# Spreading the attention values from SBUF to SBUF in sixteen transfers per group, from a value tile held twice, instead of writing them to DRAM and reading them back

## The reference

```
def reference(x, subjects, ..., conditions, ...):
    y = einsum('bct,bcd->bdt', x, w_mix1[subjects])         # 128 x 32 x 256
    q, k, v = bitlinear(y, wq), bitlinear(y, wk), bitlinear(y, wv)   # 16 heads of 16
    attn = softmax(where(causal, q @ k.T / sqrt(16), -inf))  # 32 x 32 for each head
    x = x + bitlinear((attn @ v).reshape(B, S, D), wp)
    z = einsum('bct,bcd->bdt', x, w_mix2[conditions])
    gates = top-2 of softmax(z @ router_w), normalised
    return x + sum over the two chosen experts e of
               gate_e * ((silu(z @ gate_w[e]) * (z @ up_w[e])) @ down_w[e])
```

## Time and profile before

| | |
|---|---|
| median of 3 runs | 494.92 us (494.81 to 497.31) |
| profiled execution, its own time | 493.43 us |
| its span in the profile | 491.7 us |
| TensorE busy | 341.8 us (70%) |
| VectorE busy | 261.6 us (53%) |
| ScalarE busy | 245.1 us (50%) |
| GpSimd busy | 236.3 us (48%) |
| mean granted clock of TensorE | 0.876 |

### The profile page before, as it was taken

How to read it: one execution, slowest core, us unless ns; L and a number is a source line. 1 busy time by engine, 2 the same in 40 slices (tenths; PEclk the granted TensorE clock), 3 DMA queues, 4 the chain that set the end, 5 groups by cost and what they waited for, 6 DMA issues and landing times.

```text
span 491.7 us, 11060 instructions
## 1 busy us (share of the span) xinstructions
PE 341.8 (70%) x3257; PEld 255.5 (52%) x3257; DVE 261.6 (53%) x913; ACT 245.1 (50%) x580; POOL 236.3 (48%) x248
## 2 busy tenths in 40 slices
PE   0456989989989897958755407988789888981000
PEld 0342647666756566645544306777677767760000
DVE  1635587978869797955744462333233423331531
ACT  9152778866869585845642303454444444440000
POOL 3651231246445555463556361555455555555672
PEclk9977999998999999998965657999899989997555
DMA  6506465365362715353557265544354434413994
GB/s 218 142 3 158 64 154 135 57 131 135 78 185 50 206 44 146 80 144 72 142 147 204 92 245 141 157 128 142 108 149 140 149 119 137 143 33 144 326 381 173
DMA packets 76897, 68.87 MB, mean 140 GB/s; under 512 B 41003, under 2 KB 65968, under 8 KB 76721
## 3 DMA queue, kind: packets, MB, share of 16 engines
q1 hardware_dynamic: 65200, 44.03, 36.0%
q0 software_dynamic: 7296, 20.02, 11.2%
q10 hardware_dynamic: 4352, 4.20, 2.5%
HBM read 35.36 MB, written 30.62 MB: 134 GB/s over the span
## 4 chain that ended last, share of the span: by engine, by line
PE 45%; DVE 17%; issue 9%; DMA 6%; another core or an unknown queue 5%; POOL 5%; ACT 5%; DVEq 4%; SPq 1%; POOLq 0%; ACTq 0%
PE bank L1355 12%; PE bank L1366 7%; DMA arena<-y_d 4%; PE bank L1348 3%; PE bank L1193 3%; PE bank L1244 2%; PE bank L1270 2%; PE bank L1221 2%; PE bank L1127 2%; PE bank L1142 2%; POOL arena L549 2%; DVE stats L898 2%; PE bank L1232 2%; DVE amax L851 2%
## 5 line engine op out<-in xcount | busy, mean ns | idle before, releaser
L542 POOL DMA_INDIRECT y_d<-cen,di x79 | 77.8, 985 | 77.7 <-ACT cen L748 54.0
L1057 DVE SCALAR_TENSOR_TENSOR kT<-kT,hrow,bank 128x96 f32<-128x96 f32 x79 | 24.8, 314 | 98.4 <-ACT kT L743 72.9
L502 POOL DMA_INDIRECT routed<-hrow,posi x64 | 62.8, 982 | 26.7 <-issue 16.8
L1355 PE MATMUL bank<-arena,qT 128*128 x316 | 68.6, 341 | 7.3 <-ACT qT L738 7.3
L491 POOL TENSOR_TENSOR sc<-sc,mx 128x512 f32<-128x512 f32 x32 | 33.6, 1051 | 82.1 <-DVE mx L880 82.0
L1355 PEld LDWEIGHTS bank<-arena,qT 128*128 128x128 f32 x316 | 51.4, 196 | 11.7 <-issue 11.6
L748 ACT ACTIVATE cen<-bank 128x256 f32<-128x256 f32 x79 | 30.6, 387 | 44.7 <-PE bank L1366 33.2
L1366 PE MATMUL bank<-arena,sc 96*128 x158 | 51.3, 408 | 2.0 <-issue 1.0
L1348 PE MATMUL bank<-ident,hrow 128*128 128x128 f32 x158 | 31.9, 285 | 24.5 <-DMA hrow<-routed 19.4
L738 ACT ACTIVATE qT<-bank 128x256 f32<-128x256 f32 x79 | 30.5, 386 | 22.9 <-PE bank L1348 22.7
L1348 PEld LDWEIGHTS bank<-ident,hrow 128*128 128x128 f32 x158 | 23.0, 148 | 33.8 <-DMA hrow<-routed 19.8
(11 more groups left out here) (169 smaller groups left out, 752.9 us busy)
## 6 DMA issues: line engine op xcount, KB each, us to landing
hrow<-routed SPq DMA_DIRECT2D x79, 129.0 KB
arena<-y_d SPq DMA_DIRECT2D x16, 512.0 KB, 5.4
v_d<-v_sb SPq DMA_DIRECT2D x8, 544.0 KB
vx<-v_d SPq DMA_DIRECT2D x32, 136.0 KB
X<-in_x SPq DMA_DIRECT2D x8, 512.0 KB
arena<-kT SPq DMA_DIRECT2D x64, 64.0 KB
out_x<-X ACTq DMA_DIRECT2D x16, 256.0 KB, 5.5
arena<-in_L_ffn_gate_w SPq DMA_DIRECT2D x4, 384.0 KB
```

The source lines that it names most:

```text
L502: g_.indirect_dma_start(routed, bass.IndirectOffsetOnAxis(ap=posi[g % 2][:, t, k:k + 1], axis=0), hrow[:, g % 2, t, k, :], None).then_inc( ...
L542: g_.indirect_dma_start(y_d, bass.IndirectOffsetOnAxis(ap=di[:, n:n + 1], axis=0), ye[n], None, bounds_check=Y_ROWS - 1, oob_is_err=False) ...
L1057: v.scalar_tensor_tensor(out=hh[n % 2], in0=sg[n % 2], scalar=xe[n][:, D + 1:D + 2], in1=bank[2 + n % 2][:, F:2 * F], op0=ALU.mult, op1=AL ...
L1355: last = t_.matmul(bank[2 + n][:, 0:2 * F], xeT[n][:, c, :], gu[:, c, bass.ds(expert[m + LAG - 1], 1), :].rearrange("p o f -> p (o f)"), s ...
```

## The change

The DRAM tensor `v_d`, `put_v` and its semaphore `v_put` go. `v_sb` is held twice, and group g uses `v_sb[g % 2]`. `spread_v(g)` waits for `copy_v` of its own group and for `attend(g - 1, 3)`, and then copies from `v_sb` to `vx` directly. A transfer now takes one sequence position b of a tile and one slot s, for the group's four tiles, so there are 4 x 4 = 16 of them, each of 32 x 4 x 68 numbers (34 KB). `copy_v` no longer waits for `put_v` of the group before, but for the spread of the group two before. GpSimd clears one more tile at the start.

```diff
-    v_sb = sb("v_sb", [P, TG, H, VW])
+    v_sb = [sb(f"v_sb{i}", [P, TG, H, VW]) for i in range(2)]
...
-            def put_v(g):
+            def spread_v(g):
                 if absent(g):
                     return
                 wait(sp, v_copied, g, 2, 2)
-                wait(sp, vx_in, g, 16 * SLOTS, 16 * SLOTS, lag=1)
-                sp.dma_start(v_rows, v_sb[:, :, :, :].rearrange("p t h r -> p t (h r)")).then_inc(v_put, 16)
-
-            def spread_v(g):
-                if absent(g):
-                    return
                 if g == 0:
                     sp.wait_ge(vxz_ok, 1)
-                wait(sp, v_put, g, 16, 16)
                 wait(sp, o_ready, g, TG, TG, lag=1)
-                for s in range(SLOTS):
-                    sp.dma_start(vx[s * SEQ:(s + 1) * SEQ, :, s, :], v_slots[s]).then_inc(vx_in, 16)
+                for b in range(BT):
+                    for s in range(SLOTS):
+                        sp.dma_start(vx[s * SEQ:(s + 1) * SEQ, b:TG * BT:BT, s, :],
+                                     v_sb[g % 2][b * SEQ:(b + 1) * SEQ, :, s * SLOTS:(s + 1) * SLOTS, :].rearrange("p t h r -> p t (h r)")).then_inc(vx_in, 16)
 
             def iteration(it):
-                put_v(it - 1)
                 spread_v(it - 1)
                 load_bd1(it + 2)
                 load_bd2(it - 1)
                 spread_k(it)
...
-            g_.memset(v_sb[:, :, :, :], 1.0)
+            for i in range(2):
+                g_.memset(v_sb[i][:, :, :, :], 1.0)
...
-                wait(act, v_put, g, 16, 16, lag=1)
+                wait(act, vx_in, g, 16 * SLOTS * BT, 16 * SLOTS * BT, lag=2)
...
-                    wait(pe, vx_in, g, 16 * SLOTS, 16 * SLOTS)
+                    wait(pe, vx_in, g, 16 * SLOTS * BT, 16 * SLOTS * BT)
```

More of the change, by code:

```diff
@@ L73, in build_in @@
     mix_d = [nc.dram_tensor(f"mix{i}_d", [BATCH, SEQ * SEQ], fp32, kind="Internal").ap() for i in range(2)]
-    v_d = nc.dram_tensor("v_d", [GT, H * VW], fp32, kind="Internal").ap()
     routed = nc.dram_tensor("routed", [E * PITCH, ROW], fp32, kind="Internal").ap()
@@ L202, in build_in @@
     q_ready, q_copied, k_ready, k_scaled, v_ready, v_copied = [sem(n) for n in ("q_ready", "q_copied", "k_ready", "k_scaled", "v_ready", "v_copied")]
-    kx_in, v_put, vx_in = sem("kx_in"), sem("v_put"), sem("vx_in")
+    kx_in, vx_in = sem("kx_in"), sem("vx_in")
     sc_ready, sc_copied, mx_ok, sub_ok, exp_ok = [sem(n) for n in ("sc_ready", "sc_copied", "mx_ok", "sub_ok", "exp_ok")]
@@ L277, in build_in @@
     x_v = x.rearrange("(t b) s d -> (b s) t d", b=BT)
-    v_rows = v_d.rearrange("(t p) r -> p t r", p=P)
-    v_slots = v_d.rearrange("(n j) (s r) -> s j n r", j=SEQ, s=SLOTS)
     with nc.Block() as block:
@@ L635, in copy_v @@
                     t = 2 * n + k
-                    last = a_.activation(v_sb[:, t, :, 0:HD], src[:, k * D:(k + 1) * D].rearrange("p (h r) -> p h r", h=H), ACT.Copy, scale=s_v[:, t:t + 1])
+                    last = a_.activation(v_sb[g % 2][:, t, :, 0:HD], src[:, k * D:(k + 1) * D].rearrange("p (h r) -> p h r", h=H), ACT.Copy, scale=s_v[:, t:t + 1])
                 last.then_inc(v_copied, 1)
```

## The result

The changed kernel takes 502.33 us (median of 9 runs, 498.78 to 511.4), the kernel before 497.77 us on the same chip (9 runs, 494.81 to 503.54): 1.0095 of it, with a 95% interval of 1.0062 to 1.0127. It is slower by about 1%, where no measurable change was forecast.

A forecast was written before the change was run, and what follows sets the result against it. No engine was near full, so chains of waits were taken as the limit. Span 491.7 - 5.9 (gain) + 3.9 (loss) = 489.7, plus 3.2 for a median of 492.9 us, no measurable change; range 486 to 500.

The forecast's parts named there:

- the gain: Iterations 4 to 8: without the write to `v_d`, stalls of TensorE under nearly full DMA engines shrink, 5.9 us.
- rival 2: Iterations 4 to 9: the write to `v_d` doesn't hold TensorE, gain 0, 3.9 us lost, 498.8 us; chance 0.12.
- rival 1: SP's queue: sixteen issues become the path, +9.7 us at 0.83 us an issue, 504.6 us; chance 0.15.
- The loss: SP's sixteen issues make group 1, group 7 and the first keys late: 2.0 + 1.2 + 0.7 = 3.9 us.
- An issue of SP: SP's queue: each of the sixteen transfers takes 0.71 us, with 0.47 and 0.83 as the ends.
- Keys of group 1: Iteration 1: the keys' spread, queued behind the sixteen in SP, begins at 56.3 against 55.59, 0.7 us late.
- `attend(1, 0)`: Group 1: landing takes 13.1 us from 62.44 where 11.1 are there, so it is late by 2.0 us.
- Landing: End of each set of sixteen: 2.4 us from the start of the last transfer to the work waiting for it.
- Keys of group 2: Iteration 2: issued 3.5 us late, but their scores had 3 us to spare and move by 2.0 anyway: nothing.
- Groups 2 to 6: Middle groups: 13.6 to 14.5 us are there for the values, in time by 0.7 us, no loss.
- Group 7: Its first `attend`: values late by 1.9 us, of which 1.2 count, as transposes behind wait 0.70 for ScalarE.
- Clearing: Program start: GpSimd's clearing of a second `v_sb`, 1.01 us, fits in 3.02 us idle and costs nothing.

The follow-up runs named there:

- before_again: The kernel before, run again unchanged for a second profile: 492.5 us (one run).
- write_too: The changed kernel with the old write of the values to `v_d` put back, which nothing reads: 503.44 us, 1.0156 of the kernel before.
- after_again: The changed kernel, run again unchanged on another chip: 501.63 us, 1.0022 of the kernel before.
- s_dram_first_two: The changed kernel with scatters apart, groups 0 and 1 through DRAM, second value tile cleared late: 477.23 us, 0.9634 of the kernel before.
- four_of_16: The changed kernel, groups 1 to 7 issuing only the first four of their sixteen transfers: 500.52 us, 1.0067 of the kernel before.
- s_clear_late: The changed kernel with scatters apart and the second value tile cleared in iteration 0: 481.08 us, 0.9708 of the kernel before.
- spaced_after: The changed kernel with GpSimd's scatters apart: 482.05 us, 0.9772 of the kernel before.
- two_ahead: The kernel before with scatters apart, except scatter 0 (two DMAs) put ahead of `rstd_x`: 474.63 us, 0.9604 of the kernel before.
- dram16: The kernel before, still through DRAM, with the values read back in sixteen transfers instead of four: 503.41 us, 1.0141 of the kernel before.
- s_sbuf_first_two: The changed kernel with scatters apart, second tile cleared late, only groups 0 and 1 from SBUF, the rest through DRAM: 477.73 us, 0.9644 of the kernel before.
- keys_clear: The changed kernel with the keys' spread issued ahead of the `bd` blocks and the second tile cleared in iteration 0: 504.63 us, 1.0140 of the kernel before.

## Why the prediction was wrong

Its sum was -5.9 + 3.9 = -2.0 us, for a time of 492.9 us and a range from 486 to 500; by the medians the change costs 4.6, and the time is 502.33.

**The step that failed is the gain.** It rested on one reading, that TensorE is held "while the DMA engines are nearly full", and the stall in iteration 7 is the same at a DMA share of 0.35. The write to `v_d` was priced at 1.8 us of the stall in iteration 7, 2.9 of that in 8 and 0.4 in each of 4 to 6. Measured 0 in iterations 7 and 8: 2.42 and 6.41 without the write, 2.44 and 6.42 with it; in 4 and 5 the pieces are 2.41 and 2.29 without, 2.34 and 2.18 with it. This was rival 2 (498.8 us), given 0.12; the time came out between it and rival 1 (504.6), but rival 1's condition, 0.78 us or more for an issue, wasn't met. The write was the only large transfer there, and its issue coincided with the empty 3.8 us; but the window was cut to begin there: the piece itself begins at 214.46, 2.4 us before the write is issued at 216.84 (212.83 and 215.21 in before_again). And that window had only GpSimd's scatters busy, four of the six in a row, and they were set aside as what "go on beside it". Putting them apart gave 21.8 us (495.3 to 473.54). In terms of the prediction: what the stall follows is the row of scatters, and no share of it is the write's. Whether the write costs something elsewhere is open (see write_too), but taking it away gave no gain in any run, with the scatters in rows or apart.

**The loss was right in kind and too small.**
- An issue of SP: 0.71 us taken, 0.602 the median of 128 in after_again, with gaps and stretched ones (up to 1.75) 10.3 to 11.5 us a set (12.0 at most in write_too); 11.4 forecast. Right.
- Keys of group 1: 0.7 us late forecast. They are issued 2.1 late (57.67 against 55.59), and TensorE waits 2.65 instead of 0.71. The spread began at 42.79 and not at 41.10, where the old write stood: the first scores of group 0 were already 1.5 us late (44.41 against 42.88). The clearing may have a share in it; how much, the runs don't tell.
- `attend(1, 0)`: 2.7 late with the keys' share forecast, 4.3 measured (77.82 against 73.54). The set was said to start when `vx` is free, 62.44; SP was still in keys and x until 64.4.
- Landing 2.4 us behind the start of the last issue: in s_dram_first_two SP's set ends at 222.07, its last issue began some 0.6 earlier, and the waiting `attend` starts at 223.93, 2.5 behind. Right.
- Keys of group 2, "nothing": right, the scores of group 2 wait for the `attend` ahead of them.
- Groups 2 to 6, nothing: right with the scatters apart. In the changed kernel itself their stretch is 2.6 to 4.7 us longer, for a reason that isn't known, but not by waits for their values. Group 7, 1.2: measured 1.4 with the scatters apart.
- Clearing "costs nothing": it costs 0.83 us of VectorE; first scores of group 0 start at 43.57 to 44.41 in the kernels with both clearings ahead, and at 42.96 to 43.41 in those with the second one late. But kernels with only one tile to clear have them at 42.80 to 43.97, so a price for the clearing doesn't come out of these.
- Left out altogether: the fall of the granted clock behind most of these waits (0.58 and 0.85 of full speed from 64 to 76 us in after_again). Its price is small where a later wait takes it up: in four_of_16, where `attend(1, 0)` doesn't wait, it comes 10.87 us after the first scores, against 10.39 and 10.22 before, so 0.5 to 0.7 us.

The two parts add up as far as the noise lets one see: 3.2 + 2.7 us, 5.9 of the 6.5 lost in s_clear_late, of which the rows explain 1.4 at group 7 (of the 2.7) and the late keys and `attend(1, 0)`. Why spaced_after, on another chip, shows 8.5 instead, and the change with the scatters in rows 4.6, isn't settled.

The best version is spaced, the kernel before with GpSimd's scatters apart: 0.956 [0.9508, 0.9612]. With it the way through DRAM is still the better one.

## What to carry to other kernels

A transfer that is issued where a stall stands needn't be its cause: compare the two starts first (here the stall began 2.4 us before the issue), and before pricing a gain on it, put the transfer back, or take it away alone, and look whether the stall moves. When a change adds issues to a queue that serves several stages, write out when that queue is free, issue by issue, from what stands ahead of it in the same iteration, and not from when the buffer is free. Where a change adds a wait of about 2 us or more to TensorE, price it once with the slower matmuls behind it and once without: here they followed in seven profiles of eight.

## What the runs showed of the hardware

- Four indirect scatters of GpSimd in a row (0.96 us each, 4.8 in all) go with a stop in the chain of waits of 2.2 to 2.4 us in iterations 4 to 7, six in a row (7.3 in all) with one of 6.3 to 7.6 in iteration 8 (before, before_again, after, after_again, write_too). It ends 1.0 to 1.5 us behind the row. With two in a row and other work between (spaced, two_ahead), 0.8 or none. The whole kernel gains 4.4% by taking them apart.
- An idle stretch of 1.65 to 2.65 us of TensorE ahead of the scores of group 1 is followed by matmuls at 0.61 instead of 0.39 us, at once or from the second on, in seven profiles (after_again, write_too, dram16, four_of_16, spaced_after, s_sbuf_first_two, s_clear_late), and not in one (after, 2.44 us); 0.49 to 1.00 us idle is followed by none in eight (before and s_dram_first_two among them).
- A transfer from SBUF to SBUF of 34 KB costs its issuing queue 0.60 us at the median (after_again), the same piece read from DRAM 0.43 (dram16); with the gaps between them 0.68 and 0.47.
- A clearing by GpSimd of 1 us stretches VectorE's scaling of weights beside it from 2.01 to 2.84 us (after_again); cleared later, it is 2.01 again (keys_clear, s_clear_late).
